# Higher-order linear attention on one core: a turn with three groups of 64x64 products in place of four

## The reference

```python
def _hla(x, W_q, W_k, W_v, W_o):              # b = 2, t = 2048, H = 16 heads of 64
    q = (x @ W_q).reshape(b, t, H, DK).transpose(1, 0, 2, 3)
    k = (x @ W_k).reshape(b, t, H, DK).transpose(1, 0, 2, 3)
    v = (x @ W_v).reshape(b, t, H, DV).transpose(1, 0, 2, 3)
    def step(carry, qkv):
        S_K, C_QV, G = carry
        q_t, k_t, v_t = qkv
        k_C = jnp.einsum('bhk,bhkv->bhv', k_t, C_QV)
        G = G + k_t[..., :, None] * k_C[..., None, :]
        S_K = S_K + k_t[..., :, None] * k_t[..., None, :]
        C_QV = C_QV + q_t[..., :, None] * v_t[..., None, :]
        S_C = jnp.einsum('bhkj,bhjv->bhkv', S_K, C_QV)
        o_t = jnp.einsum('bhk,bhkv->bhv', q_t, S_C - G)
        return ((S_K, C_QV, G), o_t)
    ...
    return out @ W_o
```

## Time and profile before

| | us |
|---|---|
| median of 3 runs | 1012.53 |
| the three runs | 1012.44, 1012.53, 1017.09 |
| the profiled execution | 1012.94 |
| its span, first to last instruction | 1011.2 |
| PE busy in the span | 984.6 (97%) |
| DVE busy | 618.0 (61%) |
| ACT busy | 490.3 (48%) |
| mean granted clock of PE | 0.997 of full speed |

### The profile page before, as it was taken

How to read it: one execution, slowest core, us unless ns; L and a number is a source line. 1 busy time by engine, 2 the same in 40 slices (tenths; PEclk the granted TensorE clock), 3 DMA queues, 4 the chain that set the end, 5 groups by cost and what they waited for, 6 DMA issues and landing times.

```text
span 1011.2 us, 41759 instructions
## 1 busy us (share of the span) xinstructions
PE 984.6 (97%) x18990; PEld 891.3 (88%) x18990; DVE 618.0 (61%) x1312; ACT 490.3 (48%) x941; POOL 112.8 (11%) x178
## 2 busy tenths in 40 slices
PE   8999899999999999999999999999999999989998
PEld 7888799999899989998999899999899997878997
DVE  7888877863456545655455555653654576567763
ACT  5676776643343434433444334344443345446663
POOL 2461332220000000000000000000000000022240
PEclk9999999999999999999999999999999999999999
DMA  9422212233323424432442332342443344231321
GB/s 320 146 71 84 77 50 84 84 126 126 108 87 128 149 87 127 148 109 86 131 147 91 126 125 89 126 148 86 138 140 107 108 168 154 82 105 63 125 75 52
DMA packets 76577, 115.83 MB, mean 115 GB/s; under 512 B 8816, under 2 KB 63472, under 8 KB 75376
## 3 DMA queue, kind: packets, MB, share of 16 engines
q1 hardware_dynamic: 76128, 113.15, 33.7%
q10 hardware_dynamic: 272, 0.00, 0.0%
HBM read 60.17 MB, written 52.95 MB: 112 GB/s over the span
## 4 chain that ended last, share of the span: by engine, by line
PE 94%; DVE 3%; issue 1%; DMA 1%; ACT 1%; POOL 0%; SPq 0%; POOLq 0%; DVEq 0%
PE bank L256 7%; PE bank L257 6%; PE bank L258 6%; PE bank L1252 6%; PE bank L1278 6%; PE bank L1263 5%; PE bank L1242 4%; PE bank L1312 3%; PE bank L1289 3%; PE bank L1300 3%; PE bank L854 3%; PE bank L856 3%; PE bank L1244 3%; PE bank L1243 3%; PE bank L1314 3%; PE bank L1313 3%
## 5 line engine op out<-in xcount | busy, mean ns | idle before, releaser
L1513 ACT COPY qt<-bank 128x512 f32<-128x512 f32 x64 | 37.6, 588 | 155.4 <-PE bank L258 155.4
L1653 DVE STREAM_TRANSPOSE k<-kt 128x512 f32<-128x512 f32 x64 | 43.5, 697 | 104.5 <-ACT kt L1508 55.3
L1674 DVE TENSOR_TENSOR state_s<-bank,state_s 128x256 f32<-128x256 f32 x124 | 46.8, 420 | 72.7 <-ACT ut L1526 70.7
L1508 ACT COPY kt<-bank 128x512 f32<-128x512 f32 x64 | 37.5, 587 | 109.5 <-PE bank L258 109.5
L1312 PE MATMUL bank<-wo_hi,ot_hi 128*128 128x256 f32 x256 | 74.9, 292 | 1.8 <-issue 1.2
L256 PE MATMUL bank<-ln_xhi,wq_hi 128*128 128x256 f32 x256 | 75.5, 295 | 0.0
L256 PE MATMUL bank<-ln_xhi,wk_hi 128*128 128x256 f32 x256 | 75.2, 294 | 0.0
L257 PE MATMUL bank<-ln_xlo,wk_hi 128*128 128x256 f32 x256 | 72.0, 281 | 0.6 <-issue 0.6
L257 PE MATMUL bank<-ln_xlo,wq_hi 128*128 128x256 f32 x256 | 72.4, 283 | 0.0
L258 PE MATMUL bank<-ln_xhi,wq_lo 128*128 128x256 f32 x256 | 72.4, 283 | 0.0
L258 PE MATMUL bank<-ln_xhi,wk_lo 128*128 128x256 f32 x256 | 71.7, 280 | 0.0
(11 more groups left out here) (169 smaller groups left out, 2845.2 us busy)
## 6 DMA issues: line engine op xcount, KB each, us to landing
k_rows_scratch<-k SPq DMA_DIRECT2D x32, 512.0 KB, 2.9
k<-k_rows_scratch SPq DMA_DIRECT2D x128, 128.0 KB, 2.9
u_rows_scratch<-sc_and_k SPq DMA_DIRECT2D x31, 512.0 KB, 3.4
landed<-u_rows_scratch SPq DMA_DIRECT2D x124, 128.0 KB, 2.9
ln_xn<-x_rows_scratch SPq DMA_DIRECT2D x88, 128.0 KB, 2.9
x_rows_scratch<-B_turned SPq DMA_DIRECT2D x8, 512.0 KB, 2.6
x_rows_scratch<-C_turned SPq DMA_DIRECT2D x8, 512.0 KB, 4.4
out_dram<-xres SPq DMA_DIRECT2D x16, 256.0 KB, 3.0
```

## The change

PE's order is written anew, and the waits and banks follow it. A turn now is, even and odd alike: by_states(j) | four parts of Q (even) or K (odd) | o_by_scores(j-1), u_and_s(j), change_z(j-1) | values(j) | u scores(j), key scores(j+1) | out_product(j-1). The key scores are made at the end of the turn before; change_z and out_product are one turn behind, not two. The first two parts of Q's block 1 are projected before turn 0. K, Q, change_z and the key scores share the banks WB; values use the banks OB.

```diff
-            AB, ZB, BB = WB, UB[0], UB[0]
+            AB, ZB, BB = WB, WB, UB[0]
...
             def k_bank(blk, x):
-                return (*UB[1], *WB)[x] if blk else (*UB[0], *UB[1])[x]
+                return WB[x % 2] if blk else (*UB[0], *UB[1])[x]
...
             def out_bank(i):
-                if i == CHUNKS - 1:
-                    return UB[1][0]
-                return WB[0] if i % 2 else UB[1][1]
+                return UB[1][0] if i == CHUNKS - 1 else UB[1][1]
...
                 def land_k(j):
+                    if j:
+                        sp.wait_ge(u_ready, 4 * j)
                     land_rows(rows_dram["k"], k32, k_saved, k_landed, j)
...
-                    if j % 2:
-                        sp.wait_ge(v_ready, 2 * (j + 1))
-                    elif q_block(j):
-                        sp.wait_ge(q_ready, 4 * (q_block(j) + 1))
+                    sp.wait_ge(by_state_done, 2 * (j + 2))
                     land_rows(rows_dram["u"], landed, u_saved, u_landed, j)
...
                 for j in range(CHUNKS):
+                    if j:
+                        land_u(j - 1)
                     if j + 1 < CHUNKS:
                         save_k(j + 1)
                         land_k(j + 1)
                     if j < LAST_STATE:
                         save_u(j)
-                        land_u(j)
...
                 def bs_banks_free(j, b):
                     if b == 0:
+                        if j:
+                            pe.wait_ge(b_masked, 2 * j)
+                            pe.wait_ge(v_done, 2 * j - 1)
                         if j > 1:
                             pe.wait_ge(z_added, 2 * (j - 1))
-                        elif j:
-                            pe.wait_ge(b_masked, 2 * j)
-                    elif j % 2:
-                        if j == CHUNKS - 1:
-                            pe.wait_ge(gelu_done, 6)
-                        else:
-                            pe.wait_ge(k_done, 4 * k_block(j) + 2)
-                    elif j:
-                        pe.wait_ge(x_added, j - 1)
-                    if j > 1:
-                        pe.wait_ge(o_low, 2 * (j - 2) + b + 1)
...
+                    else:
+                        if j:
                             pe.wait_ge(v_done, 2 * j)
+                        if j > 1:
+                            pe.wait_ge(x_added, j - 1)
...
                     for b in range(B):
                         bs_banks_free(j, b)
                         by_states(j, b)
...
                     pe.wait_ge(by_state_done, 2 * (j + 1))
+                    if j:
+                        pe.wait_ge(v_done, 2 * j)
+                        pe.wait_ge(b_masked, 2 * j)
+                        o_by_scores(j - 1)
+                    pe.wait_ge(a_masked, 2 * (j + 1))
                     pe.wait_ge(krow_done, 2 * (j + 1))
                     u_and_s(j)
...
+                        change_z(j - 1)
+
+                    for x in range(2):
+                        if j:
+                            pe.wait_ge(o_low, 2 * (j - 1) + x + 1)
+                        values(j, x)
+
                     pe.wait_ge(ut_done, 4 * (j + 1))
                     if j < LAST_STATE:
                         pe.wait_ge(s_added, 4 * j + 3)
                     scores_of(j, lambda p, h, b: ut[half(h), b, p, :], BB, b_ready)
...
+                        key_scores(j + 1)
+
+                    if j:
+                        if j < LAST_STATE:
+                            pe.wait_ge(s_added, 4 * (j + 1))
+                        out_product(j - 1)
...
+                    if j:
+                        store_k_rows(j)
+                    for x in range(4):
+                        if x == 3 and j:
+                            store_u_rows(j - 1)
...
+                            store_k(blk, x)
...
+                        high(j - 1)
                     store_ut(j)
...
+                    for x in range(2):
+                        store_v(j, x)
```

More of the change, by code:

```diff
@@ L1425, in tensor @@
                         by_states(j, b)
-                    for x in range(2):
-                        pe.wait_ge(a_masked, 2 * j + x + 1)
+                    if j == 0:
+                        key_scores(0)
+                    for x in range(2 if j == 0 else 0, 4):
+                        if x < 2:
+                            pe.wait_ge(a_masked, 2 * j + x + 1)
+                        elif blk:
+                            pe.wait_ge(q_done if even else k_done, 4 * blk + x - 1)
                         if not blk:
-                            up(x if even else 6 + x)
+                            up(x if even else 4 + x)
                         elif even:
@@ L1460, in tensor @@
                     scores_of(j, lambda p, h, b: ut[half(h), b, p, :], BB, b_ready)
-                    if j < LAST_STATE:
-                        pe.wait_ge(s_added, 4 * (j + 1))
-                    for x in range(2):
-                        if not even:
-                            values(j, x)
-                        elif blk:
-                            project_q(blk, 2 + x)
-                        else:
-                            up(2 + x)
+                    if j + 1 < CHUNKS:
+                        if j:
+                            pe.wait_ge(z_added, 2 * j)
+                        else:
+                            pe.wait_ge(q_done, 8)
+                        key_scores(j + 1)
+                    if j:
+                        if j < LAST_STATE:
+                            pe.wait_ge(s_added, 4 * (j + 1))
+                        out_product(j - 1)
                 j = CHUNKS
-                first_group(j)
-                pe.wait_ge(v_done, 2 * j)
-                out_product(j - 2)
                 for b in range(B):
@@ L1517, in store_v @@
                     act.wait_ge(v_ready, 2 * j + x + 1)
[L1518 removed]
+                    nc.scalar.copy(v_all[:, j % 2, x * BLK:(x + 1) * BLK], bank[OB[x]][:, :]).then_inc(v_done, 1)
                 def store_ut(j):
@@ L1610, in scalar @@
                         ln.act_high_rows(act, 0, moves(0, 0))
-                    if not even:
-                        store_v(j, 0)
-                        if j == CHUNKS - 1:
-                            act.wait_ge(v_ready, 2 * CHUNKS)
-                            ln.act_high_rows(act, 1, moves(1, 0))
-                        store_v(j, 1)
-                    elif blk:
-                        for x in range(2):
-                            store_q(blk, 2 + x)
-                    else:
-                        hide(2, 3)
+                    elif j == CHUNKS - 1:
+                        ln.act_high_rows(act, 1, moves(1, 0))
                 hide(FC)
@@ L1749, in vector @@
                 dve.wait_ge(masks_done, 2)
+                dve.wait_ge(state_zero, 2)
+                mask_scores(0, lambda h: sc_a[:, :, h, :], a_bank(0), a_ready, a_masked)
                 for j in range(CHUNKS):
[L1751 removed]
                     if j > 1:
[L1753 to L1771 removed]
+                        add_out(j - 2)
                     if norm_of(j + 1):
@@ L1798, in vector @@
                         ln.dve_statistics(dve, block_of(j + 1), 0, nd)
-                    if j == CHUNKS - 1:
+                    if j + 1 < CHUNKS:
+                        turn_keys(j + 1)
+                    if j >= CHUNKS - 2:
+                        for n in range(4):
+                            low((j - CHUNKS + 2) * 4 + n)
+                    if j:
+                        out_low(j - 1)
+                    if j < LAST_STATE:
+                        add_s(j)
+                    if j:
+                        add_z(j - 1)
+                    if j < LAST_STATE:
+                        turn_u(j)
+                    mask_scores(j, lambda h: sc_b[:, h, :, :], BB, b_ready, b_masked)
+                    if norm_of(j - 1):
+                        chunk_low(norm_of(j - 1) - 2)
+                    elif block_of(j - 1) == 0:
+                        ln.dve_low_rows(dve, 0, nd)
+                    elif j == CHUNKS - 1:
                         ln.dve_low_rows(dve, 1, nd)
+                    if j + 1 < CHUNKS:
+                        dve.wait_ge(u_saved, 16 * (j + 1))
+                        mask_scores(j + 1, lambda h: sc_a[:, :, h, :], AB, a_ready, a_masked)
+                    else:
                         ln.dve_statistics(dve, 0, 1, nd + 1)
-                add_z(CHUNKS - 2)
                 add_out(CHUNKS - 2)
```

130 lines of the change are left out of this document (28 added, 102 removed).

## The result

| | before | after |
|---|---|---|
| median of 4 runs, us | 1014.25 | 1029.01 |
| lowest and highest | 1012.44, 1017.09 | 1027.05, 1030.15 |
| profiled execution, its span | 1012.94, 1011.2 | 1030.02, 1028.3 |
| ratio, with 95% interval | | 1.0139 [1.0117, 1.0161] |

The change makes the kernel 1.4% slower. The forecast was 1016, in a range of 1004 to 1026: the sum was +3.8 us where the two profiled executions stand 17.1 apart. The medians stand 14.8 apart; all that follows about single terms is read from the two profiled executions, and so has to explain 17.1.

What follows compares the result with a forecast made beforehand. PE, with 94% of the chain, bounds the kernel; other engines and DMAs count only where PE waits. On 1012.9, -8.1 - 0.8 + 1.2 + 8.2 + 1.8 + 1.5 = +3.8 gave 1016.7, median 1016, range 1004 to 1026.

Steps and rivals of the forecast that it cites:

- the copy of Q: Ahead of turn 0: the pair of Q parts projected early covers PE's wait for this copy, -0.8 us.
- The switches (-8.1): PE's turns: 31 fewer stays in 64x64 products, at 0.26 us each, give -8.1 us.
- A wait that is there today: by_states, batch 1, waits for add_out: 0.08 us in even turns already, now also in 15 odd ones, +1.2 us.
- The wait for add_out (8.2 and 1.8): Odd turns: add_out late behind the save of u, +8.2 us; x block still landing in 7 odd turns, +1.8.
- the formula K - 2.7: Odd turns: add_out's lateness in us, where K is the time of the save of the keys.
- The layout's 6.3: Odd turns, SP's queue: us from the start of the keys' landing until u is saved; bounds 5.7 and 6.6.
- In even turns ... I take nothing (bound: 0.3 each, +4): Even turns: u is saved 0.7 us early, so add_out adds nothing; bound 0.3 us each, +4 in all.
- Rest: x block landing in 7 odd turns, +1.8 us; turn 29's weight load and turns 30 and 31, +1.5 (0 to 4).
- C: Rival, same wait for add_out but larger: late by 1.1 us in mean odd turns, 0.2 in even; 1027 us, chance 0.24.
- A: Rival: the save of u meets a drained queue, add_out isn't late, only the switches count; 1006 us, chance 0.27.
- D: Rival: the 0.26 us belongs to a hidden wait, so joining groups gives nothing; 1024 us, chance 0.07 with others.
- The rule weighed: DMA time is 2.0 us plus bytes by 436 GB/s, whatever stands ahead; by it add_out would not be late.

Runs made afterwards that it cites:

- Runs 4 and 5: Changed kernel with turn 0's key-row copy (ACT) and save of u (SP) moved earlier, 1028.31 us; then also add_out ahead of the key-score mask, 1012.40 us.
- k_all: Changed kernel with add_out ahead of the key-score mask, turn 0 reordered on ACT and SP, and the 1 MB weight load behind turn 29's landing of u: 1011.16 us.
- Run 8: Changed kernel with turn_u(j) ahead of add_z(j-1) on DVE: 1030.57 us, ratio 1.015.
- run 7: k_all with the first half of the values between u_and_s and change_z, one more stay in 64x64 products a turn: 1021.78 us, ratio 1.0073.
- Run 6: The run of k_all, which issues the weight load behind the landing of u in turn 29, among other repairs to the changed kernel: 1011.16 us, ratio 0.9963.
- k_start: Changed kernel with turn 0 alone altered: ACT copies key rows after two Q parts, SP saves u ahead of the keys' landing: 1028.31 us, ratio 1.0137.
- k_own_mem: Changed kernel with the turned u in its own memory in turns 0 to 29, so the key-score mask needn't wait for its save: 1015.52 us, ratio 1.0012.
- k_turn_first: The kernel of Run 8: changed kernel with turn_u(j) ahead of add_z(j-1) on DVE: 1030.57 us, ratio 1.015.

## Why the prediction was wrong

**The step that failed is the start.** The prediction took -0.8 for the copy of Q and never laid out turns 0 and 1, though the changed order of ACT and SP was at hand. They cost +5.3: 6.1 off a sum that was 13.3 short. Runs 4 and 5 show the order to be the cause: two steps moved bring by_states(2) to 272.30 and 272.25 (273.19 in k_all), level with before's 272.89. And the prediction priced a wait of PE at its own length: the clock behind it was no term of the sum. In turn 1 it cost 2.6. Run 8 has the same order at the start, its K parts of turn 1 take 5.87 at a granted clock of 1.00, and by_states(2) comes at 275.75: so some 2.4 to 2.6 of the 5.3 are the clock, and the rest the waits.

The other shortfalls are waits in odd turns 3.1, turn 29 2.2, the end of the span 1.0, waits and slow projections behind odd turns 1.1; the stops and rounding make the difference. With +5.3 in place of -0.8 the forecast would have been 1022, 7 below the median.

**The switches (-8.1), with the +1.2 of "A wait that is there today": met, partly by luck.** The turns should have been 0.18 and 0.26 shorter; they are 0.16 and 0.29, and the layout's 19.9 was met. But run 7 puts a stay at 0.38, not 0.26, and by_states takes 2.20, not 2.11: two terms were too small, and they cancel.

**The wait for add_out (8.2 and 1.8): right in place and mechanism; the term that was too small is the save of u.** The save of the keys issued in turn 5, in the DMA view (KB, us to landing):

```profile
k_rows_scratch<-k SPq DMA_DIRECT2D x1, 512.0 KB, 3.6
```

The one of turn 25, and the save of u behind it:

```profile
k_rows_scratch<-k SPq DMA_DIRECT2D x1, 512.0 KB, 3.8
...
u_rows_scratch<-sc_and_k SPq DMA_DIRECT2D x1, 512.0 KB, 4.8
```

All odd turns of after, in us (K is the time of the save of the keys, as in the prediction, U that of the save of u in the same turn):

| odd turn | 1 | 3 | 5 | 7 | 9 | 11 | 13 | 15 | 17 | 19 | 21 | 23 | 25 | 27 |
|---|---|---|---|---|---|---|---|---|---|---|---|---|---|---|
| K | 3.3 | 2.8 | 3.6 | 2.8 | 4.0 | 2.9 | 3.3 | 3.3 | 2.8 | 4.1 | 2.7 | 2.9 | 3.8 | 2.8 |
| U | 3.4 | 3.0 | 3.4 | 3.3 | 4.6 | 3.3 | 4.9 | 3.6 | 3.7 | 4.7 | 3.2 | 4.9 | 4.8 | 3.1 |
| wait in the next turn | 0 | 0 | 0.65 | 0 | 1.56 | 0 | 1.27 | 0.84 | 0 | 1.62 | 0 | 1.11 | 3.4 | 0 |

The mean K of these turns is 3.2, which is what the forecast used (2.65 and 0.55 on top). (The page's median over all 32 saves is 3.5, against the 2.9 of the earlier trace rows; that is the even turns, where the save is now issued right behind the four landings of u.) By the formula K - 2.7 the waits sum to 7.3, measured 10.45. The layout's 6.3 from landing to saved holds 3.6 for U; in turns 9, 13, 19, 23 and 25 it took 4.6 to 4.9. It is K and U together that tell the turns apart: where they sum to 6.9 or more PE waits, where to 6.5 or less it doesn't. Turn 1, with 6.7, is itself 6.4 us longer than a plain one, so its add_out was not late. In turn 25 SP also took 2.8 to issue the four landings, where it took 1.7 in turn 9, and by_states and the projections behind it ran at a granted clock of 0.84 and 0.88.

**"In even turns ... I take nothing (bound: 0.3 each, +4)"** measured 3.1, inside the bound as a sum, but not in each turn: 2.8 of it stand behind turns 4 (1.53), 14 and 24, where a save was long (u 5.2, keys 5.8, u 4.3). In turn 4 a 512 KB save of x was issued 0.4 behind the save of u; but so it was in turns 8, 12, 16 and 20, where u took 2.8 to 3.0, so that isn't the cause by itself.

**"Rest", turn 29: 1.5 (0 to 4).** It became 3.7, inside its bound. Run 6 shows that this was an order, too: behind the landing the load costs next to nothing in that turn.

**The rivals.** C named this mechanism and gave 1027, with the wait in mean odd turns at 1.1; measured it is 0.7 (10.45 by 15). Its sign, by_states above 3 us in most even turns, was seen in 6 of the 14 even turns from 2 on. That the time came out at 1029 nevertheless is the start's doing, so C was close for a reason that it didn't have. A is refuted by the waits of DVE, D by run 7.

**The rule weighed** was the Trainium skill, page "DMA: Bandwidth & Descriptors", section "Anatomy of one DMA": an estimate of 3.2 us for 512 KB. The section gives its fit for DMAs that GpSimd issues; these saves are SP's. Of the 31 saves of u in after, 23 took 2.8 to 3.8, around the estimate, and eight 4.3 to 5.2. With 3.2 for U the formula would be K - 3.1 and give 3.7 us of waits, with the prediction's 3.6 it gives 7.3, measured 10.45: not following the rule was right.

**What stays open.** Why PE stops for 1.2 us in by_states(1), and for 0.3 to 1 us every 100 us, was not tried; the trace calls it "issue". The former is there in k_all too, whose by_states(1) takes 3.76. Nor is it shown why some saves are long. The prediction put it down to instruction loads. In the trace before, every save of the keys above 2.9 overlaps such a load, and the seven that overlap none took 2.6 to 2.8; but the loads are on queue q8 and the saves on q1, and in after, saves of the keys in even turns took 3.3 to 3.7 with no load beside them. No run moves the loads.

## What to carry to other kernels

Where an engine's list has a wait for a DMA, look at what stands behind it and who needs that: moving one short step ahead of the wait gave 10.5 us, where doing the DMA sooner lost 8. Lay out the first and the last turns of a changed loop by themselves; they have other neighbours, and here the first two held 6.1 of the 13.3 us of error. A gain of 0.2 us a turn is real, but one late transfer cost 0.65 to 3.4, as much as three to fifteen such turns give, so first see to it that the new order has slack for the longest transfer in the trace, not for the median.

## What the runs showed of the hardware

- The clock behind a wait. In turns 1 to 29 of the nine changed kernels eleven by_states took 1.8 us or more above its 2.20. Eight times the projections behind it were slow: 8.47 and 6.62 in turns 1 and 26 of after, 7.43 in turn 6 of k_start, 6.5 to 7.4 in the others, where 5.9 is normal. Three times, with 2.1, 2.6 and 3.3 above, they were not. Below 1.8 none was slow, apart from short stops inside them. So the length of the wait alone doesn't tell. The stretch behind by_states(1), which took 1.9 more in k_own_mem and 3.3 more in k_turn_first (the first number behind the last bracket is the granted clock):

```profile
258.00:265.40 7.40, 7.40 (x54) 7.26 (x51) 0.71 (x1) 2.50 (x5) 0.00 (x0) 0.77 0.26 73
...
257.40:263.30 5.90, 5.90 (x52) 5.77 (x53) 1.23 (x2) 2.54 (x5) 0.00 (x0) 1.00 0.32 89
```

- The 512 KB save of the keys took 2.7 to 4.1 in the odd turns of after, the save of u 2.8 to 5.2; behind a 1 MB load landings of 128 KB took 5.6 to 6.3.
- A stay in 64x64 products cost 0.38 us here: 0.09 going in, 0.11 coming out, and the rest at the end of the groups, which the pitch alone doesn't show.
